# Five weight slots for six in a four-block decoder stack: a moved hidden half, two moved value projections, earlier bias loads

## The reference, cut to what matters

```
L0, L1: h = LN(x); x += attn(h, h) @ Wo + bo        16 heads of 64
        h = LN(x); x += attn(h, ctx) @ Wo + bo
        h = LN(x); a, g = split(h @ Wp + bp); x += (a * gelu(g)) @ Wf + bf
L2:     x += attn(LN(x), ctx) @ Wo + bo             16 heads of 64
L3:     self attention (causal and padding mask), cross attention (padding mask),
        16 heads of 16; then x += gelu(LN(x) @ W1 + b1) @ W2 + b2
attn(h, c) = softmax((h Wq)(c Wk)^T * scale) (c Wv)
```

## Time and profile before

| | |
|---|---|
| median of 3 runs | 1585.03 us (1585.01 to 1589.24) |
| the profiled execution | 1586.22 us, of which the traced span is 1584.3 us |
| granted PE clock, mean | 0.992 |
| busy: PE, PE weight load | 1523.8 us (96%), 1331.7 us (84%) |
| busy: DVE, ACT, POOL | 938.6 us (59%), 1025.1 us (65%), 825.5 us (52%) |
| DMA | 67.12 MB, mean 42 GB/s |

### The profile page before, as it was taken

How to read it: one execution, slowest core, us unless ns; L and a number is a source line. 1 busy time by engine, 2 the same in 40 slices (tenths; PEclk the granted TensorE clock), 3 DMA queues, 4 the chain that set the end, 5 groups by cost and what they waited for, 6 DMA issues and landing times.

```text
span 1584.3 us, 37770 instructions
## 1 busy us (share of the span) xinstructions
PE 1523.8 (96%) x13974; PEld 1331.7 (84%) x13974; DVE 938.6 (59%) x2522; ACT 1025.1 (65%) x2944; POOL 825.5 (52%) x1380
## 2 busy tenths in 40 slices
PE   8999999999999999999999999999999988899988
PEld 7888788888789898888888889888888877777778
DVE  7666554545457655654545566654455568867773
ACT  6566666667661655776666682566666678778871
POOL 3666357676553544536766754246676742533321
PEclk8999999999999999999999999999999999999999
DMA  5332110001110100210010111110100110011000
GB/s 164 110 112 91 65 41 18 19 18 45 42 45 30 61 25 2 74 54 19 18 36 18 43 62 40 50 42 20 34 19 18 52 58 20 17 33 34 19 1 24
DMA packets 40500, 67.12 MB, mean 42 GB/s; under 512 B 8064, under 2 KB 15008, under 8 KB 40320
## 3 DMA queue, kind: packets, MB, share of 16 engines
q1 hardware_dynamic: 39888, 64.68, 12.9%
q10 hardware_dynamic: 432, 0.04, 0.0%
HBM read 59.16 MB, written 5.54 MB: 41 GB/s over the span
## 4 chain that ended last, share of the span: by engine, by line
PE 84%; DVE 7%; ACT 4%; issue 3%; POOL 1%; DMA 0%; SPq 0%; DVEq 0%; ACTq 0%
PE pG L1238 50%; PE pO L1238 12%; PE pG L1433 12%; PE pS L1238 10%; ACT P L1614 1%; DVE KF L1762 1%; PE pG L1489 1%; DVE W L1692 1%; DVE nmax L1744 0%; DVE bn L1674 0%; DVE nmax L1759 0%; DVE full L1822 0%; ACT QF_hi L1558 0%; DVE hid_hi_f L1706 0%; SPq L1194 0%
## 5 line engine op out<-in xcount | busy, mean ns | idle before, releaser
L1883 POOL TENSOR_SCALAR P<-P,rinv 112x375 f32<-112x375 f32 (+1 forms) x640 | 325.8, 522 | 239.4 <-DVE rinv L1768 238.6
L1614 ACT ACTIVATE P<-pS,nmax 112x375 f32<-112x375 f32 (+1 forms) x640 | 308.3, 498 | 100.2 <-DVE nmax L1744 100.2
L1238 PE MATMUL pG<-hT_hi,W 128*128 128x224 f32 (+1 forms) x1312 | 301.0, 309 | 8.8 <-DVE hid_hi_f L1706 2.2
L1627 ACT ACTIVATE PT<-pG 125x336 f32<-125x336 f32 (+1 forms) x448 | 198.3, 469 | 86.7 <-PE pG L1433 86.3
L1238 PEld LDWEIGHTS pG<-hT_hi,W 128*128 128x128 f32 x1312 | 225.5, 194 | 21.4 <-DVE hid_hi_f L1706 3.1
L1433 PE MATMUL pG<-ident,P 112*125 112x112 f32 (+1 forms) x1472 | 225.3, 277 | 12.6 <-POOL P L1883 6.5
L1744 DVE TENSOR_REDUCE nmax<-pS 112x1 f32<-112x375 f32 (+1 forms) x448 | 228.2, 549 | 7.6 <-PE pS L1238 6.4
L1433 PEld LDWEIGHTS pG<-ident,P 112*125 112x125 f32 (+1 forms) x1472 | 185.5, 176 | 44.1 <-issue 8.6
L1238 PE MATMUL pG<-src,W 128*128 128x376 f32 (+1 forms) x956 | 220.5, 353 | 0.4 <-ACT whole_f L1562 0.2
L1238 PE MATMUL pG<-hT_lo,W 128*128 128x224 f32 (+1 forms) x656 | 196.3, 299 | 0.0
L1238 PEld LDWEIGHTS pG<-src,W 128*128 128x128 f32 (+1 forms) x956 | 158.8, 189 | 27.8 <-issue 25.3
(11 more groups left out here) (139 smaller groups left out, 2959.1 us busy)
## 6 DMA issues: line engine op xcount, KB each, us to landing
wraw<-wts SPq DMA_DIRECT2D x110, 256.0 KB, 2.6
src<-ctx_split SPq DMA_DIRECT2D x64, 282.0 KB, 3.1
ctx_split<-hid_lo_t SPq DMA_DIRECT2D x8, 564.0 KB, 3.6
whole_f<-wts SPq DMA_DIRECT2D x14, 256.0 KB, 6.4
V<-ctxT SPq DMA_DIRECT2D x8, 376.0 KB, 4.2
src_half<-ctx_split SPq DMA_DIRECT2D x21, 94.0 KB, 3.2
bo_b<-bo SPq DMA_DIRECT2D x10, 112.0 KB, 3.3
out<-x SPq DMA_DIRECT2D x8, 112.0 KB, 1.9
```

The source lines that it names most:

```text
L1238: return nc.tensor.matmul(o, l, r, start=first, stop=last)
L1614: ins = act.activation(o, pS[U % 4][0:T, i * n:(i + 1) * n], ACT.Exp, bias=nmax[:, r, i:i + 1], accum_out=rsum[:, r, i:i + 1])
L1627: act.activation(o[0:sh.krows, 0:n], g[0:sh.krows, 0:n], ACT.Copy).then_inc(pt_ready, 1)
L1883: ins = pool.tensor_scalar(o, o, rinv[:, r, i:i + 1], st.nscale, ALU.mult, ALU.mult)
```

## The change

- The slots of `W` become five: item i takes slot i mod 5 and so waits for item i-5. All slot numbers in `make_stages` and `FFS` follow. `W` shrinks by 16 KB of each partition, which nothing else takes up.
- `hid_lo_2` moves from over W slot 3 to the place of `KF` and `QF`, and `half_free` of stage 6 therefore also waits for stage 6's last transposes and last `av`.
- The two value projections of stage 2's batch 0 leave the end of the first feed-forward's tail and go behind stage 2's first score set.
- The bias loads become six events of four DMAs, `not_before` 60, 75, ... 135 in the planner's time, so they fall into stage 0. (The planner's duration for one goes from 0.7 to 0.25.)

```diff
@@ make_stages, FFS, SLOT_OF (L0c shown; the other stages are renumbered alike)
-    L0c = dict(i=1, ..., q=(4, 0, W), k=(5, 0, W), v=(0, 0, W), o=(1, 0, C), ...
+    L0c = dict(i=1, ..., q=(4, 0, W), k=(0, 0, W), v=(1, 0, W), o=(2, 0, C), ...
-FFS = {1: FF(2, 3, 4, 2, 2, 0, "erf"), 3: FF(1, 2, 3, 5, 5, 16, "tanh"), 6: FF(None, 0, 1, 9, 9, 32, "erf")}
+FFS = {1: FF(3, 4, 0, 2, 2, 0, "erf"), 3: FF(4, 0, 1, 5, 5, 16, "tanh"), 6: FF(None, 0, 1, 9, 9, 32, "erf")}
-SLOT_OF = [0, 1, 2, 3, 4, 5, 0, 1, 2, 3, 4, 5, 0, 1, 2, 3, 4, 5, 0, 1, 2, 3, 4, 5, 0, 1, 2, 3, 4, 5, 0, 1]
+SLOTS = 5
+SLOT_OF = [i % SLOTS for i in range(32)]
@@ fill
+        if s == 2 and b == 0 and i == 0:
+            out += [Ev("v", 2, 0, 0), Ev("v", 2, 0, 1)]
@@ tail
-        values = [Ev("v", nxt.i, 0, 0), Ev("v", nxt.i, 0, 1)]
+        values = []
...
-    return out + opening.pop(0) + opening.pop(0) + values
+    return out + opening.pop(0) + opening.pop(0) + (values if s == 3 else [])
@@ duration
-        return .7 if k == "bias" else .06
+        return .25 if k == "bias" else .06
@@ plan
-    for s in (5, 6):
-        task("sp", Ev("bias", s), not_before=250. + 200. * (s - 5))
-    task("pool", Ev("bq"), ("sp", Ev("bias", 6)), not_before=500.)
+    for n in range(6):
+        task("sp", Ev("bias", 0, n), not_before=60. + 15. * n)
+    task("pool", Ev("bq"), ("sp", Ev("bias", 0, 5)), not_before=500.)
@@ program
-        W = sb("W", [128, 6, 2, 2048], F32R)
+        W = sb("W", [128, SLOTS, 2, 2048], F32R)
-        hid_lo_2 = nc.alloc_sbuf_tensor_at("hid_lo_2", [128, 8, CHUNK], F32R, offset=w_place + 3 * 4 * 2 * 2048)
-        hid_lo_2f = nc.alloc_sbuf_tensor_at("hid_lo_2f", [128, 8 * CHUNK], F32, offset=w_place + 3 * 4 * 2 * 2048)
+        hid_lo_2 = nc.alloc_sbuf_tensor_at("hid_lo_2", [128, 8, CHUNK], F32R, offset=k_place)
+        hid_lo_2f = nc.alloc_sbuf_tensor_at("hid_lo_2f", [128, 8 * CHUNK], F32, offset=k_place)
@@ half_free
-            wait(eng, pieces, piece_no[Ev("wo", 5, B - 1) if s == 6 else Ev("ff2", s, 3)])
+            if s == 6:
+                wait(eng, transposed, BASE[6] + B * H)
+                wait(eng, attended, av_no[Ev("av", 6, B - 1, 3)])
+                wait(eng, pieces, piece_no[Ev("wo", 5, B - 1)])
+            else:
+                wait(eng, pieces, piece_no[Ev("ff2", s, 3)])
@@ the SP program
-                    for i in range(3 * s - 15, 3 * s - 12):
-                        for t in range(2):
-                            for k in range(2):
-                                four = bsm[:, i, t + 2 * k:t + 2 * k + 1].rearrange("(r j) c -> r j c", r=4)
-                                sp.dma_start(bias_c[64 * t:64 * t + 64, i, k:k + 1], four[:, 0:16, :],
-                                             allow_slow_non_contiguous=True).then_inc(bias_in, 16)
+                    for t in range(2):
+                        for k in range(2):
+                            four = bsm[:, b, t + 2 * k:t + 2 * k + 1].rearrange("(r j) c -> r j c", r=4)
+                            sp.dma_start(bias_c[64 * t:64 * t + 64, b, k:k + 1], four[:, 0:16, :],
+                                         allow_slow_non_contiguous=True).then_inc(bias_in, 16)
```

More of the change, by code:

```diff
@@ L30, in make_stages @@
                qscale=0.125, escale=1.0, nscale=1.0)
-    L0c = dict(i=1, self_=False, small=False, ln=1, res=1, q=(4, 0, W), k=(5, 0, W), v=(0, 0, W), o=(1, 0, C),
+    L0c = dict(i=1, self_=False, small=False, ln=1, res=1, q=(4, 0, W), k=(0, 0, W), v=(1, 0, W), o=(2, 0, C),
                qscale=0.125, escale=1.0, nscale=1.0)
-    L1s = dict(i=2, self_=True, small=False, ln=3, res=3, q=(5, 0, W), k=(0, 0, W), v=(1, 0, W), o=(2, 0, C),
+    L1s = dict(i=2, self_=True, small=False, ln=3, res=3, q=(1, 0, W), k=(2, 0, W), v=(3, 0, W), o=(4, 0, C),
                qscale=0.125, escale=1.0, nscale=1.0)
-    L1c = dict(i=3, self_=False, small=False, ln=4, res=4, q=(3, 0, W), k=(4, 0, W), v=(5, 0, W), o=(0, 0, C),
+    L1c = dict(i=3, self_=False, small=False, ln=4, res=4, q=(0, 0, W), k=(1, 0, W), v=(2, 0, W), o=(3, 0, C),
                qscale=0.125, escale=1.0, nscale=1.0)
-    L2c = dict(i=4, self_=False, small=False, ln=6, res=6, q=(4, 0, W), k=(5, 0, W), v=(0, 0, W), o=(1, 0, C),
+    L2c = dict(i=4, self_=False, small=False, ln=6, res=6, q=(2, 0, W), k=(3, 0, W), v=(4, 0, W), o=(0, 0, C),
                qscale=1.0, escale=1.0, nscale=0.125)
-    L3s = dict(i=5, self_=True, small=True, ln=7, res=7, q=(2, 0, W), k=(2, 512, W), v=(3, 0, 512), o=(3, 1024, C),
+    L3s = dict(i=5, self_=True, small=True, ln=7, res=7, q=(1, 0, W), k=(1, 512, W), v=(2, 0, 512), o=(2, 1024, C),
                qscale=0.25, escale=1.0, nscale=1.0)
-    L3c = dict(i=6, self_=False, small=True, ln=8, res=8, q=(4, 0, 512), k=(5, 0, 512), v=(5, 1024, 512), o=(4, 1024, C),
+    L3c = dict(i=6, self_=False, small=True, ln=8, res=8, q=(3, 0, 512), k=(4, 0, 512), v=(4, 1024, 512), o=(3, 1024, C),
                qscale=1.0, escale=-0.25, nscale=1.0)
```

## The result

The changed kernel takes 1593.84 us in the median of four runs (1591.6 to 1595.2), the one before 1585.02 beside it. The ratio is 1.0047, 95% interval 1.0029 to 1.0065: slower by 7.5 us, that is 1592.5 us on the scale of the prediction, where 1587.7 was forecast with 1592.5 as the upper end. The medians themselves are 8.8 us apart, and a second comparison (run 5) gave 1.0035. The profiled execution took 1594.82 us, 8.6 us more than the one of before. Single executions of one and the same kernel scatter here by several us (the kernel before: 1581 to 1594 over all its runs), so terms of 1 to 4 us are read from the traces and only the totals from the medians.

What follows compares the result with a forecast made beforehand. PE, busy 96% of the span, was taken as the bound, with DVE in stage 5. Terms -2.9 - 0.6 (stage 0) + 2.0 + 3.2 + 1.0 = +2.7 on 1585.03 gave 1587.7 us; own range 1585.5 to 1590, wider 1583.0 to 1592.5.

Steps and rivals of the forecast that it cites:

- rival C: Stage 5: POOL holds DVE, all four chunk subtracts take 1.53 us; +7.4 in all, 1592.4 us; chance 0.18.
- Bias loads out of stage 1, -2.9: Stage 1: twelve bias issues leave SP's queue ahead of a weight chunk; the stretch falls from 19.90 to 17.00 us.
- Rival D: Stage 1: bias loads are hidden anyway, so the gain there doesn't come; +5.6 in all, 1590.6 us; chance 0.10.
- Four chunks fewer in stage 0, -1.2: Stage 0: chunks 20 to 23 leave it, and 1.2 us of a 1.55 us PE wait go; ends 0 and -1.55.
- Bias loads into stage 0, +0.6: Stage 0: three of six bias events stand ahead of a context-row load, 0.2 us of PE each; ends 0 and 2.3.
- Opening of stage 2, +2.0: Stage 2: value weights' slot comes free late, PE waits 2.0 us for the second values; ends 0 and 3.3.
- Last four chunks in stage 5, +3.2: Stage 5: chunks 124 to 127 move to batches 5 and 6, adding DVE work ahead of a score set; ends 1.3 and 5.0.
- Rival B: Stage 5: the chunks fall into DVE's and PE's idle time and no clock is lost; -1.5, 1583.5 us; chance 0.24.
- Clock, +1.0: Stages 2 and 5: half clock behind two new or longer PE waits, 0.3 of up to 1.7 us each; ends 0 and 3.4.
- Nothing, for `hid_lo_2` in the place of `KF`: Stage 6: the added waits are on work already ended before, so the buffer's move costs 0.
- a half-rate stretch in stages 0 to 4: Stages 0 to 4: a stretch of PE at half clock there would make the forecast wrong.

Runs made afterwards that it cites:

- run 5: The changed kernel unaltered, measured a second time against the kernel before: ratio 1.0035 (1.0018 to 1.0052).
- run 2: The kernel before, six slots, with all 24 bias loads moved to about 230 us: 0.9982 of the kernel before.
- run 3: The changed kernel, five slots, with the bias loads back at their old times: 1.0054 of the kernel before, 1595.0 us.
- run 4: The changed kernel, five slots, with its bias loads at 230 us instead of stage 0: 1.0031 of the kernel before, 1591.3 us.
- run 6: The changed kernel, five slots, with the last four weight chunks held back to stage 6: 1.0006 of the kernel before, 1588.0 us.
- run 1: The kernel before, six slots, with only the 24 bias loads moved into stage 0 in six events of four: 0.9992 of the kernel before.
- run 8: The changed kernel, five slots, with the last two chunks of stage 2's value weights put earlier: 1.0041 of the kernel before, 1591.4 us.

## Why the prediction was right or wrong

The direction and the places were right. The sum was +2.7 where +7.5 (interval 4.6 to 10.3) was measured; two terms were too small, and four held. The forecast's own range, 1585.5 to 1590, left the result out. That the wider range just reaches 1592.5 is luck: it went that far only for rival C, whose mechanism did not come. Slower by over 0.3%, as it came out, had a chance of 0.29.

*Bias loads out of stage 1, -2.9:* measured -3.0 in the changed kernel and -2.96 in run 2. Rival D fell. What the Trainium skill says in "DMA: Bandwidth & Descriptors", section "Issuing engines are not separate DMA queues", that starting a DMA usually takes little time beside the DMA itself, would have put this term near 0; the traces differ, for twelve tiny ones held the queue for 6.96 us ahead of a chunk, and moving them gave 3.0.

*Four chunks fewer in stage 0, -1.2:* measured -1.24 and -1.22 in runs 3 and 4. The wait of 1.55 us is 0.31 in the changed kernel, as foretold.

*Bias loads into stage 0, +0.6:* this step failed. I gave each of three events 0.2 us of PE time. A load of context rows behind four issues comes 2.8 us later, ACT stands in its order for 1.0, 2.3 and 3.5 us more, and behind it stand its copies and exponentials; PE lost 1.7 to 3.6 us in the five traces that have the loads there. My upper end for it, 2.3, took one event in full; right would have been each of the three against the wait that ACT already had.

*Opening of stage 2, +2.0:* PE's wait is 2.19 us, and the table load was early as assumed. The term holds; the clock behind it is counted below.

*Last four chunks in stage 5, +3.2:* PE's wait grew by 2.87 us, and 0.6 was lost ahead of it, 3.5 together. Rival B fell: DVE had no room for the chunks. Rival C's mechanism, all four subtracts of 1.53 us, did not come: they took 0.68, 0.83, 0.88 and 0.68. Its time of 1592.4 was the one measured, by another cause. By the Trainium skill, "SBUF — State Buffer", section "Who interferes with whom", such a subtract contends with a GpSimd instruction that reads SBUF; the one of 0.88 us ran beside one of POOL, so at most 0.2 us of it are that, and no run here separates it.

*Clock, +1.0:* this step failed most. I put 0.3 of 1.7 us on each of two waits. Both brought it, in every trace: 4.0 - 2.2 = 1.8 us in stage 2, and 5.7 - 2.9 = 2.8 us in stage 5, where the clock was at 0.61 and 0.50 over two windows of 3.4 us. Together 4.6, above my upper end of 3.4, since I took one stretch of 3.4 us behind each wait as the most, and in stage 5 it was 6.8. The prediction also counted a half-rate stretch in stages 0 to 4 among the signs that it is wrong, while this term allowed one in stage 2; there was one in stage 2 and, by chance, one in stage 0.

The profile before gave no sure sign of it. Behind the 3.20 us wait of stage 5 the clock fell, behind the 3.22 us wait of stage 0 (above) it did not; behind 1.36 and 1.06 us in stage 1 it did not, and behind 1.36 us at the opening of stage 6 it did:

```profile
1383.70 1.11 PE L1238 MATMUL pS<-hid_hi_t,hid_lo_t 16*112 16x376 f32 x12 [1.36 <-DVE nmax L1762]
```
```profile
1383.90:1387.30 3.40, 3.40 (x41) 2.62 (x38) 1.67 (x6) 1.18 (x3) 0.17 (x1) 0.51 0.00 0
```

*Nothing, for `hid_lo_2` in the place of `KF`:* no run has it alone. From the last score sets of stage 6 to the last piece the five-slot traces differ from the kernel before by -0.9 to +0.8 us and the six-slot ones, which have it in the old place, by -1.4 to +0.8, so no cost of it shows.

With the terms as measured: -3.0 - 1.2 + 1.7 to 3.6 + 2.2 + 3.5 + 4.6 = 7.8 to 9.7, against 7.5 and 5.6 by the two ratios (1.0047, 1.0035) and 8.6 by the profiled executions. That the sum meets the first trace's 8.7 is in part chance: its half clock in stage 0 (+1.6) and 6.8 us of it instead of 3.4 behind stage 5's wait of 3.2 us at batch 4 (some +1.4) are offset by 1.2 us in its first 37 us, 1.0 between stages 2 and 5 and 1.6 in the tail.

Why did the bias loads in stage 0 cost 3.6 us in one trace and 1.7 in the other? The clock was at 1.00 in both. Of the difference 0.9 us lie behind the first context rows, where ACT waited alike (1.32 and 1.42 us) but DVE's subtract took

```profile
65.75 1.66 DVE L1815 TENSOR_TENSOR hid_lo_t<-V,hid_lo_t 64x376 fp32r<-64x376 f32 x1 [1.16 <-ACT hid_lo_t L1582]
```

beside POOL's subtract on the same tile, and 0.60 us in the other trace; PE then waited 1.31 and 0.33 us for DVE's `KF`. Where DVE's took long (here and in run 6, 1.66 and 1.62 us), POOL's took 0.99 and 1.00; where DVE's was short (0.55 to 0.60 us, in runs 1, 5 and 8), POOL's took 1.29 to 1.34. One of the two gives way, and which one varies from trace to trace. Another 0.6 us lie at the second rows (ACT's wait 2.79 and 2.22 us) and 0.4 at the third (5.28 and 4.83). What decides each of these stays open.

## What to carry to other kernels

A DMA issue that "only moves" must be priced at what stands behind it on its new queue place: by the waits which the engine there already has, since each of them can grow by the full time of the issues or more (here by 1.0, 2.3 and 3.5 us for issues of 2.8). On an engine that is nearly full in a stretch (DVE 18.9 of 20 us here), added work goes to the time one for one, and a new wait on PE must be priced with the half clock behind it, here nearly as much again. The length of the wait alone does not tell whether it comes: it came in five of five traces behind 2.19 us and in five of five behind 3.78 us, in nine of 14 behind 3.2 us in stage 0, and in twelve of 14 behind 1.36 us at the opening of stage 6. So take the clock at the same places from several traces of the kernel before, and give the term a range that holds the longest stretch seen (6.8 us here). A buffer less is paid for where its last reader and the next writer's first reader are close, so look at the schedule's tightest reuse and where the displaced loads go, not at the mean load.

## What the runs showed of the hardware that was not expected

PE's granted clock fell behind the waits of 2.19 and 3.78 us in every trace that had them (five each), and did not behind those of 1.01 and 0.90 us at the same places. Elsewhere the same wait in the same code brought half clock in some executions only: 3.2 us in stage 0 in nine of 14, 1.2 us in stage 1 in four of 14, 1.36 us at the opening of stage 6 in twelve of 14. At the wait of 3.2 us in stage 5's batch 4 it came in all ten traces with that wait, for 3.4 us in four and 6.8 us in six. In stage 5 the length went with the moment: where the clock fell before the wait had ended it stayed at half for 6.8 us (six of the ten at batch 4, all five at batch 7), where it fell 0.5 to 1.7 us behind the wait's end, for 3.4 us (the other four). Tiny DMAs (64 values of 4 bytes) held SP's queue for 0.58 us each in the earlier trace rows and 0.70 in a group of four. ACT's table load of 1.28 us started at once behind the copy before it, 4.4 us ahead of the exponential it serves, which itself waited 3.14 us.
